# A running maximum scanned in two steps an edge, with the passed maximum read out of the same scan (graph attention, one Trainium2 core)

## What is computed

```
s = leaky_relu(xl[src] + xr[dst])
e = einsum('eho,ho->eh', s, a)
m = segment_max(e, dst)
ex = exp(e - m[dst])
denom = segment_sum(ex, dst)
out = segment_sum(xl[src] * (ex / (denom[dst] + 1e-16)), dst)
```

## Time and profile before

| | |
|---|---|
| median of 3 runs | 6350.81 us (6348.14 to 6351.27) |
| the profiled execution, its own time | 6349.54 us |
| its span | 6347.7 us |
| attention layer one, turns | about 235 to 1670 us |
| attention layers two and three, turns | about 1810 to 3210 us, 3360 to 4750 us |
| edge-attribute layer | from about 4850 us |

### The profile page before, as it was taken

The page is one execution under the profiler, slowest core; times in us unless marked ns, Lnnn a source line. Parts: engine busy times, 40 slices in busy tenths (PEclk is TensorE's granted clock), DMA queues, the critical chain, the costliest instruction groups (busy, mean ns, idle before and its releaser), DMA issues.

```text
span 6347.7 us, 100679 instructions
## 1 busy us (share of the span) xinstructions
PE 5801.3 (91%) x26479; PEld 4876.6 (77%) x26479; DVE 5002.1 (79%) x7708; ACT 4444.1 (70%) x6153; POOL 4666.4 (74%) x4884
## 2 busy tenths in 40 slices
PE   2899999999799999999969999999986999999996
PEld 1688787787578888888858888888864888888884
DVE  8699999999769999999958999999985444444443
ACT  1588888878468888888837888888874666666663
POOL 3777777777677777777767777777767777777775
PEclk9999999999799999999979999999997999999997
DMA  9677777777445555555535555555553444444442
GB/s 392 228 245 243 242 243 246 243 243 245 136 148 176 178 177 178 177 178 176 178 96 167 178 177 178 177 178 180 177 162 88 146 145 146 146 145 148 146 145 69
DMA packets 453003, 1153.13 MB, mean 182 GB/s; under 512 B 158796, under 2 KB 224832, under 8 KB 416876
## 3 DMA queue, kind: packets, MB, share of 16 engines
q1 hardware_dynamic: 281624, 927.58, 40.5%
q0 software_dynamic: 156944, 173.32, 14.7%
q10 hardware_dynamic: 14404, 51.92, 2.1%
HBM read 754.04 MB, written 398.35 MB: 182 GB/s over the span
## 4 chain that ended last, share of the span: by engine, by line
POOL 41%; issue 20%; PE 13%; DVE 11%; ACT 8%; DMA 3%; SPq 2%; DVEq 1%; POOLq 0%; ACTq 0%
POOL sb_xl L552 36%; PE pG L641 12%; ACT sb_v_in L766 3%; DVE pG L1245 3%; POOL sb_hot_f L552 3%; DVE sb_s_run L1287 2%; ACT sb_hot L766 2%; ACT sb_turn_out L766 2%; DMA sb_xl<-xl_table,sb_idx 2%; POOL marks L556 1%; SPq L364 1%; DVE sb_e_in L1311 1%; DVE sb_lr L1309 1%; DVE sb_s L1307 1%; ACT pB L766 1%
## 5 line engine op out<-in xcount | busy, mean ns | idle before, releaser
L641 PE MATMUL pG<-sb_xl_parts,sb_hot 128*128 128x476 f32 (+1 forms) x25074 | 5507.8, 378 | 221.0 <-ACT sb_xl L766 121.5
L641 PEld LDWEIGHTS pG<-sb_xl_parts,sb_hot 128*128 128x128 f32 x25074 | 4683.2, 189 | 1041.7 <-issue 422.8
L552 POOL DMA_INDIRECT sb_xl<-xl_table,sb_idx x4481 | 4271.2, 953 | 1381.0 <-issue 1352.7
L766 ACT ACTIVATE sb_hot<-sb_wide 128x1792 fp32r<-128x1792 bf16 (+1 forms) x796 | 1485.8, 1880 | 267.1 <-DMA sb_wide<-hots 227.0
L1245 DVE COPY_PREDICATED pG<-sb_pick_turn,pG 128x272 f32<-128x272 int32 (+9 forms) x2388 | 1110.6, 465 | 551.5 <-PE pG L641 455.6
L1287 DVE TENSOR_TENSOR_SCAN sb_s_run<-pB,sb_v_in 128x272 f32<-128x272 f32 (+3 forms) x1470 | 1095.9, 773 | 220.6 <-ACT sb_v_in L999 219.2
L766 ACT ACTIVATE sb_turn_out<-sb_s_run 128x1088 f32<-128x1088 f32 (+2 forms) x399 | 831.9, 2086 | 6.0 <-DVE sb_s_run L1287 6.0
L1284 DVE TENSOR_TENSOR_SCAN pB<-sb_same_c,pB 128x1024 f32<-128x1024 f32 x294 | 672.1, 2286 | 0.2
L766 ACT ACTIVATE sb_xl<-pG 128x136 f32<-128x136 f32 (+4 forms) x838 | 251.6, 303 | 502.6 <-DVE pG L1245 381.9
L766 ACT ACTIVATE sb_v_in<-sb_v_g 128x1024 f32<-128x1024 f32 x291 | 600.7, 2064 | 0.0
L1307 DVE TENSOR_TENSOR sb_s<-sb_xl,pB 128x1024 f32<-128x1024 f32 x294 | 354.5, 1206 | 143.5 <-DMA sb_xl<-xl_table,sb_idx 141.3
(11 more groups left out here) (261 smaller groups left out, 2309.4 us busy)
## 6 DMA issues: line engine op xcount, KB each, us to landing
state_rows<-sb_turn_out SPq DMA_DIRECT2D x294, 576.0 KB
sb_wide<-hots SPq DMA_DIRECT2D x149, 1120.0 KB
sb_mark<-marks SPq DMA_DIRECT2D x294, 512.0 KB
sb_wide<-hots SPq DMA_DIRECT2D x149, 896.0 KB
sb_xl<-xl_table,sb_idx POOLq DMA_INDIRECT x4481
sb_wide<-codes SPq DMA_DIRECT2D x50, 1120.0 KB
hots<-sb_wide SPq DMA_DIRECT2D x50, 1120.0 KB, 4.3
marks<-sb_hot_f SPq DMA_DIRECT2D x32, 1568.0 KB
```

The lines of the kernel that those rows point to most:

```text
L552: return pool.indirect_dma_start(out=dst, out_offset=None, in_=table, in_offset=bass.IndirectOffsetOnAxis(ap=index, axis=0))
L641: product = pe.matmul(pG[:, bank + a - lo, 0:GB * n], hot[k][:, m, a * P:(a + 1) * P], rows[:, :, 0:n], start=(m == 0 and part == 0), stop ...
L766: return act.activation(out, in_, ACT.Copy)
```

## The change

Every head's row gets 33 columns instead of 17: the carried one, and then for each edge two, a "passed" and a "reached" column. In a passed column the mark is added and the operand of the maximum is -3e38, so that the scan leaves the passed maximum there; in a reached column the mark is 0 and the operand is the score. One scan over 4 x 33 = 132 columns so leaves both maxima, the addition L1316 is gone, and the subtraction reads its first operand partly from the scores and partly from the scan's output, with a step of two columns. Scores, scan outputs of both turns of a pair, and a gap of one column lie in one tile (`maxima`), so that one access pattern can reach both. The zeros of the reached marks and the -3e38 are written once, at the start.

```diff
 G1 = G + 1
+GX = 2 * G + 1
+HX = H * GX
+LOWEST = -3.0e38
...
-        neg_h = sb("neg_h", [P, H, G1])
+        neg_h = sb("neg_h", [P, H, GX])
...
-        e_in = sb("e_in", [P, 2, H, G1])
-        m_run = sb("m_run", [P, 2, H, G1])
+        maxima = sb("maxima", [P, 2 + 4 * HX])
+        e_in = maxima[:, 0:HX].rearrange("p (h x) -> p h x", h=H)
+        m_run = [maxima[:, at:at + HX].rearrange("p (h x) -> p h x", h=H) for at in (HX + 1, 2 * HX + 1)]
+        m_last = [m_run[k][:, :, GX - 1:GX] for k in range(2)]
+
+        def reached(ap):
+            return ap[:, :, 1:GX].rearrange("p h (g t) -> p h g t", t=2)[:, :, :, 1]
+
+        def passed(ap):
+            return ap[:, :, 1:GX].rearrange("p h (g t) -> p h g t", t=2)[:, :, :, 0]
+
+        def terms_and_passed(k):
+
+            both = maxima[:, 2:2 + 2 * (k + 1) * HX].rearrange("p (a r) -> p a r", a=2)[:, :, 0:HX]
+            return both.rearrange("p a (h x) -> p a h x", h=H)[:, :, :, 0:2 * G].rearrange("p a h (g t) -> p a h g t", t=2)[:, :, :, :, 0]
...
-        K_TURN, K_ENDS, K_NODE = 5, 10, 4 * GROUPS
+        K_TURN, K_ENDS, K_NODE = 4, 10, 4 * GROUPS
...
-                act.activation(neg_h[:, :, :], same[:, bass.ds(turn, 1), :].to_broadcast([P, H, G1]), ACT.Identity, bias=neg_col[:, 0:1], scale=-NEG).then_inc(s_e_carried, 1)
+                act.activation(passed(neg_h), same[:, bass.ds(turn, 1), 1:G1].to_broadcast([P, H, G]), ACT.Identity, bias=neg_col[:, 0:1], scale=-NEG).then_inc(s_e_carried, 1)
...
-                copy(turn_out[:, k, :, V:ROW], m_run[:, k, :, 1:G1].rearrange("p h g -> p g h"))
+                copy(turn_out[:, k, :, V:ROW], reached(m_run[k]).rearrange("p h g -> p g h"))
...
+            dve.memset(reached(neg_h), 0.0)
+            dve.memset(neg_h[:, :, 0:1], NEG)
+            dve.memset(passed(e_in), LOWEST)
...
-                e_turn = e_in[:, 0, :, 1:G1]
+                e_turn = reached(e_in)
...
-                done(dve.tensor_tensor_scan(m_run[:, k].rearrange(flat3), neg_h[:].rearrange(flat3), e_in[:, 0].rearrange(flat3),
+                done(dve.tensor_tensor_scan(m_run[k].rearrange(flat3), neg_h[:].rearrange(flat3), e_in.rearrange(flat3),
                                             0.0, ALU.add, ALU.max)); steps_done()
-                done(tt(e_in[:, 1, :, 1:G1], m_run[:, k, :, 0:G], neg_h[:, :, 1:G1], ALU.add)); steps_done()
-                tt(wf_arg[:], e_in[:, :, :, 1:G1], blocks(m_run[:, k, :, 1:G1], 2), ALU.subtract).then_inc(s_args, 1)
+                tt(wf_arg[:], terms_and_passed(k), blocks(reached(m_run[k]), 2), ALU.subtract).then_inc(s_args, 1)
```

More of the change, by code:

```diff
@@ L890, in attention_turn @@
                     copy(v_turn[:, 0:C, :].rearrange("p c g -> p g c"), v_g[:].rearrange("p g (h o) -> p g o h", h=H)).then_inc(s_v, 1)
-                    copy(e_in[:, 0, :, 0:1], m_run[:, k, :, G:G1])
+                    copy(e_in[:, :, 0:1], m_last[k])
                     spread_neg(turn + 1)
@@ L1377, in attention_layer @@
                 ts(a_turn, a_all[:, bass.ds(l * C, C)], 1.0 - SLOPE, None, ALU.mult)
-                dve.memset(e_in[:, 0, :, 0:1], NEG)
+                dve.memset(e_in[:, :, 0:1], NEG)
                 dve.memset(v_in[:, :, 0:1], 0.0)
@@ L1425, in run_ends @@
                 done(cp(fin_s[:, :], s_run[:, :, G]))
-                cp(fin_m[:], blocks(m_run[:, 1, :, G], HO)).then_inc(s_fin, 1)
+                cp(fin_m[:], blocks(m_last[1].rearrange("p h x -> p (h x)"), HO)).then_inc(s_fin, 1)
                 last()
```

## The result

| | before | with the change |
|---|---|---|
| median of 20 runs each | 6349.78 us (6346.92 to 6351.77) | 6360.69 us (6354.63 to 6368.31) |
| ratio | 1 | 1.0017, interval 1.0011 to 1.0023 |
| layer one, first to last L1307 (now L1327) | 1426.3 us | 1435.6 us |

The change makes the kernel 10.9 us slower. The forecast was 6337.5 us, 13.3 us faster. The profiled execution of the changed kernel took 6368.31 us, longer than its 19 others.

A forecast was written before the change was run, and what follows sets the result against it. VectorE was taken to bound layer one, GpSimd's gathers layers two and three. Saving 259 - 132 = 127 ns over 98 + 7 turns gave 13.3 us off the median 6350.81, so 6337.5 us; range 6334.5 to 6345.5 us.

The forecast's parts named there:

- What bounds layer one: Layer one: VectorE, busy 1387.72 of 1410 us, works through its own list and waits for nobody.
- The prices: VectorE's turn: addition gone saves 259 ns, longer scan costs 132 ns, two-column step costs 0; 127 ns shorter.
- A: Rival for VectorE's saving: all of the gain arrives, 6336.9 to 6338.8 us; chance 0.70.
- B: Rival in layer one's wide turns: ScalarE's answer becomes late, 6.2 us lost again, 6343.7 us; chance 0.10.
- C: Rival at L1312 and the subtraction: 8-byte step costs; half price about 6353 us, chance 0.09; full 6369 us, 0.03.
- E: Rival for all layers: VectorE's pace counts in each, 37.3 us gained, 6313.5 us; chance 0.03.
- What is late next: Layer one's pair of turns: becomes 29.19 us, GpSimd's 0.64 us slack shrinks to some 0.4, ScalarE tightest with 0.06 left.
- Rival D: Layer one: GpSimd was the pace all along, its pair stays 29.4 us, only edges gain, 6349.9 us; chance 0.05.
- The seven edge turns: Edges of layers two (3 turns) and three (4): the chain passes through VectorE, so each gains 0.127 us.
- S: Experiments' theory, VectorE's scan: the longer scan itself, with both operands in SBUF, holds GpSimd's gathers.
- P: Experiments' theory, layer one: VectorE's builds and GpSimd's gathers hold each other up; a turn 124 ns shorter moves that.

The follow-up runs named there:

- z1_reduce_before: The kernel before with each one-hot build of layer one replaced by a reduction of about the same length; 6347.37 us, 0.9996 of before.
- x4_longer: The kernel before with a chained fill of two columns as one more VectorE step a turn; 6377.88 us, 1.0043 of before.
- z3: The kernel before with the two pieces of a build swapped in size, 4 blocks first and 3 behind; 6362.59 us, 1.0019 of before.
- z2_reduce_after: The changed kernel with each one-hot build of layer one replaced by a reduction of about the same length; 6337.29 us, 0.9979 of before.
- x3_short: The kernel before without the addition L1316, the scan kept at 68 columns, the passed maximum left out; 6353.91 us, 1.0004 of before.
- z4_four_after: The changed kernel with the two pieces of a build swapped in size, 4 blocks first and 3 behind; 6340.90 us, 0.9986 of before.
- x1_layout: The kernel before with two unused SBUF gaps that put later tiles at the changed kernel's addresses; 6350.83 us, 1.0001 of before.

## Why the prediction was wrong

- *What bounds layer one*: half read. VectorE was full and is the pace of the kernel before (z1_reduce_before: without any hold it gains 3 us, most of it because the reductions are 58 ns a pair shorter). That GpSimd was full as well I did not look up; I added 23 usual gathers and called the rest slack.
- *The prices*: right. Scan 434 ns against 431; the two-column step free (277 and 294 ns; the subtraction's 337 ns before belong to that execution's meeting, as it seems, for the unchanged instruction takes 293 to 295 in x4_longer, z1 and z3). 259 - (434 - 299) = 124 ns a turn against 127. One bound was added wrongly: with a scan at 140 ns more, A comes to 6338.3 us, not 6338.8. Rivals B, C and E did not occur.
- *What is late next*: **the step that failed.** The text: "I read this as GpSimd held by that build; then the 0.64 us are slack that shrinks to some 0.4." The first half is right but for the 1536-column build that shares in it, and z1 and z2 show it. The second isn't: the hold doesn't shrink with VectorE's turn. It is what the meeting of 4 builds, 2 scans and 23 gathers gives, 0.74 us a pair before, 0.92 and 0.99 in the two traces after, 0.48 with the pieces swapped, 0 with the reductions. Nor did the prediction ask whether the longer scan itself holds gathers. GpSimd could follow at 29.2 us only with under 0.5.
- *Rival D* came nearest: GpSimd with a pair that doesn't get shorter, VectorE waiting for gathers. But it had the hold as a fixed price, so that the edges would still gain (6349.9 us); the hold grew. No rival had a time above before through GpSimd; the only slower case was C's, at 0.03.
- *The seven edge turns*: no gain seen. Layers two and three are 1392.4 and 1392.3 us in z1, 1392.2 and 1392.7 in z2, where 0.9 us in all was forecast, within what such layers scatter.
- *S is a part of P*, and in the changed kernel not a small one: a gather that starts 0.07 us after the start of the long scan is held 0.17 us; one that starts 0.05 us after the start of the 68-column scan is held 0.05 us (x3_short, 932.49). In the changed kernel this is 7.2 us of layer one, most of what the hold grew by. It is neither needed (x3_short has the short scan, and 43.1 us are held) nor does it follow from the scan alone (z2_reduce_after 0.1 us, z4_four_after 0.4 us). How the 9.3 us of layer one divide between builds and scan is not shown.

Why the builds, scans and gathers meet where they do in each kernel stays open; I have no rule that would have told 3 blocks from 4 without a run. Nor is it known what makes the usual gather of an execution 944 or 947 ns.

## What to carry to other kernels

When two engines show hardly a wait over the same stretch, take of each the busy time plus the number of its instructions times the fixed gap: if both sums fill it, neither has slack, and a shorter list on one is a gain only if the other can follow. Time an engine loses to being held is not slack to be spent; it depends on where the instructions meet, and an edit of pace, even one that removes work, can change it for the worse. So, where such holds exist, test a change with a second cut of the contending work (here one digit) before it is judged: this one is worth -22, +11 or -10 us as the builds are cut 4 + 3 or 3 + 4, or hold nobody.

## What the runs showed of the hardware

- A gather that starts in a VectorE build (`tensor_scalar`, bf16) ends about 0.13 us earlier than the sum of the build's rest and its own free length (changed kernel, 910.71: rest 0.47 us, held 0.33), and one that starts within 0.04 us of the build's start is held 0 to 0.06 us. A gather that started first is held as well: 923.73 began 0.38 us before the 1920-column build and took 1.22 us. So neither blocks the other for a whole instruction. The Trainium skill (SBUF — State Buffer, section "Who interferes with whom") has an exclusive lock in which the one that issues first blocks the other "for the whole instruction"; the measurement differs.
- A VectorE scan with two operands in SBUF held an indirect gather by 0.17 us (906.79). The Trainium skill (same section) says that an instruction with two SBUF inputs contends with a GpSimd instruction that reads SBUF; of `tensor_tensor` it infers, and says so, that it leaves the making of descriptors alone. It names no scan; the 0.17 us speak against carrying that inference over to one.
- Executions whose usual gather is 947 instead of 944 ns were longer: of the changed kernel by 6.7 us (6368.31 against 6361.63, with layer one alike), of the old program by 20.4 us (x1_layout's 6369.97, at other addresses, against 6349.54), of which 7.0 in layer one. The 13.4 us of 4481 x 3 ns is neither; what 3 ns do depends on where GpSimd is the pace and on the meeting.
